# A graph network with routed experts and two attention layers on one core: output bias in bf16 parts, attention rows from two banks, one square root, and each strong result added ahead of the next group sum

## What is computed

```python
h = x @ W_in + b_in                                   # 6250 x 256
for l in range(3):
    agg = segment_sum(h[src], dst) / deg
    logits = concatenate([h, agg]) @ router_W[l] + router_b[l]
    gates = softmax of the two largest of 8 logits, 0 elsewhere
    weak = relu(agg @ weak_W[l] + weak_b[l])          # 4 experts, 256 -> 256
    sh = relu(agg @ strong_W1[l] + strong_b1[l])      # 4 experts, 256 -> 512
    strong = sh @ strong_W2[l] + strong_b2[l]         # 512 -> 256
    moe = sum over the 8 experts of gate * result
    h = h + sigmoid(h @ conf_W[l] + conf_b[l]) * moe
x1 = layernorm(x + h @ W_out + b_out)                 # 6250 x 128
y = gat(elu(gat(x1, 4 heads of 32)), 1 head of 128)   # attention over the edges
return layernorm(x1 + y)
```

## Time and profile before

| | us |
|---|---|
| median of 3 runs | 8288.14 |
| lowest, highest | 8262.08, 8299.24 |
| the profiled execution | 8303.62 |
| its span in the trace | 8302.0 |
| busy in the span: POOL, PE, DVE, ACT | 4148.2, 3593.2, 3261.6, 1275.6 |
| mean granted PE clock | 0.681 |

### The profile page before, as it was taken

How to read it: one execution, slowest core, us unless ns; L and a number is a source line. 1 busy time by engine, 2 the same in 40 slices (tenths; PEclk the granted TensorE clock), 3 DMA queues, 4 the chain that set the end, 5 groups by cost and what they waited for, 6 DMA issues and landing times.

```text
span 8302.0 us, 58045 instructions
## 1 busy us (share of the span) xinstructions
PE 3593.2 (43%) x11996; PEld 2114.2 (25%) x11996; DVE 3261.6 (39%) x6283; ACT 1275.6 (15%) x2738; POOL 4148.2 (50%) x4324
## 2 busy tenths in 40 slices
PE   3127777676567666665666666662000000000000
PEld 2124333344433333334433333331000000000000
DVE  2224444343333333333333333324444444454553
ACT  1002222222122222221222222221000000000000
POOL 5654445454544344445344444334655565666555
PEclk6558888788677877776778787876555555555555
DMA  2332222222322222223121212112212121211111
GB/s 66 88 107 65 72 64 76 72 74 64 94 63 63 58 68 62 68 63 96 54 62 56 61 55 62 55 33 48 50 45 47 47 48 39 46 46 45 45 43 42
DMA packets 259368, 500.84 MB, mean 60 GB/s; under 512 B 104427, under 2 KB 146340, under 8 KB 258874
## 3 DMA queue, kind: packets, MB, share of 16 engines
q0 software_dynamic: 176592, 446.04, 20.5%
q1 hardware_dynamic: 56234, 33.56, 1.5%
q10 hardware_dynamic: 26432, 20.02, 0.7%
HBM read 464.44 MB, written 34.88 MB: 60 GB/s over the span
## 4 chain that ended last, share of the span: by engine, by line
PE 33%; issue 24%; another core or an unknown queue 18%; DVEq 10%; DVE 6%; ACT 3%; POOL 1%; ACTq 1%; DMA 0%; SPq 0%; POOLq 0%
PE ps_w1a L1942 7%; PE ps_w1b L1942 6%; PE ps_gate L1967 5%; PE ps_wide L1967 4%; PE ps_weak_a L1954 3%; PE ps_weak_b L1954 3%; DVE ps_wide L1382 2%; DVEq L1414 2%; PE ps_weak_a L1926 1%; DVEq L1427 1%; DVEq L1354 1%; DVEq L1424 1%; ACT weak L1611 1%; DVEq L363 1%
## 5 line engine op out<-in xcount | busy, mean ns | idle before, releaser
L655 POOL DMA_INDIRECT ring<-hidden_tab,stage x2400 | 2316.0, 965 | 2792.0 <-DVE ps_wide L967 1779.5
L655 POOL DMA_INDIRECT ring<-gat_tab,stage x1600 | 1530.4, 956 | 1143.7 <-issue 651.0
L973 DVE TENSOR_TENSOR ps_wide<-ps_wide,ring 128x1024 f32<-128x1024 f32 x418 | 516.2, 1235 | 544.3 <-issue 537.1
L1942 PE MATMUL ps_w1a<-agg_team_t,wbuf 128*128 128x512 f32 (+1 forms) x1248 | 632.5, 625 | 201.1 <-ACT strong L1590 108.6
L1942 PE MATMUL ps_w1b<-agg_team_t,wbuf 128*128 128x512 f32 (+1 forms) x1248 | 591.8, 595 | 51.5 <-issue 46.9
L1967 PE MATMUL ps_gate<-wbuf,strong 128*128 128x256 f32 x2400 | 578.3, 387 | 14.4 <-issue 14.2
L1967 PE MATMUL ps_wide<-wbuf,strong 128*128 128x256 f32 x2304 | 555.8, 384 | 62.7 <-issue 62.2
L2078 PE MATMUL ps_w1a<-ident,agg_team_t 128*128 128x128 f32 x28 | 7.8, 434 | 1242.9 <-DVE agg_team_t L1460 666.8
L1967 PEld LDWEIGHTS ps_gate<-wbuf,strong 128*128 128x128 f32 x2400 | 443.2, 195 | 131.8 <-issue 65.8
L1967 PEld LDWEIGHTS ps_wide<-wbuf,strong 128*128 128x128 f32 x2304 | 419.8, 192 | 143.7 <-issue 66.2
L977 DVE SCALAR_TENSOR_TENSOR ps_wide<-ring,before_cut,ps_wide 128x256 f32<-128x256 f32 x556 | 243.5, 485 | 478.4 <-issue 462.1
(11 more groups left out here) (409 smaller groups left out, 4659.7 us busy)
## 6 DMA issues: line engine op xcount, KB each, us to landing
ring<-hidden_tab,stage POOLq DMA_INDIRECT x2400
ring<-gat_tab,stage POOLq DMA_INDIRECT x1600
hidden_tab<-h_res ACTq DMA_DIRECT2D x24, 512.0 KB, 3.0
hidden_tab<-h_res SPq DMA_DIRECT2D x12, 512.0 KB
wbuf<-in_L_gnn_strong_W SPq DMA_DIRECT2D x6, 1024.0 KB
wbuf<-in_L_gnn_strong_W SPq DMA_DIRECT2D x12, 512.0 KB
gat_tab<-h_res ACTq DMA_DIRECT2D x19, 272.0 KB
wbuf<-in_L_gnn_weak_W SPq DMA_DIRECT2D x6, 512.0 KB
```

What stands on the lines that cost most here:

```text
L655: return pool.indirect_dma_start(out=ring[:, b, 0:width], out_offset=None, in_=table, in_offset=bass.IndirectOffsetOnAxis(ap=stage[:, half ...
L973: nc.vector.tensor_tensor(wide_s, wide_s, rows(u), ALU.add).then_inc(ring_free, 1)
L1942: last = mm(ps_w1[c % 2][:, 0:size * P], w1_w[:, k, s, c * P:(c + 1) * P], agg_team_t[:, k, 0:size * P], start=k == 0, stop=k == 1)
```

## The change

Four things, in five engines' programs:

1. **Output bias.** `b_out` is no longer multiplied in fp32 by a row of ones. It is loaded on three partitions (`bias_out`), split by `bias_parts` into three bf16 rows of a 128 x 128 tile `out_parts` that is otherwise 0, and each group's projection starts with one bf16 product of ones with it.
2. **Attention rows.** The eight score columns are a product of their own into a second bank, so the features of four groups fill one bank. ACT copies a batch in three activations and drains once. The stores are issued by SP in its pass for the first attention layer, each after `row_done`.
3. **One square root.** ACT computes Sqrt instead of Ln and Exp, after the last team's state copies instead of before them, and DVE takes the reciprocal.
4. **Order on DVE.** In every team step of all three expert layers `add_strong(s - 1)` and a drain stand ahead of `gather_next(s)`. In the last-but-one and last steps (few or no next groups) the same lines run with little or nothing to sum.

```diff
@@ parameters, SP
-        ones_row = sb("ones_row", [1, P])
-        b_out_r = sb("b_out_r", [1, IN])
+        out_parts = sb("out_parts", [P, IN], BF16)
+        bias_out = agg_flat[:, P:P + IN]
-        PAR_DMAS = 4 + 5 + 4 * LAYERS + 2 * (2 + 2 * HEADS)
+        PAR_DMAS = 3 + 8 + 4 * LAYERS + 2 * (2 + 2 * HEADS)
-            par(b_out_r[:], b_out.rearrange("(a n) -> a n", a=1))
             for row in PART_ROWS:
                 par(bias_in[row:row + 1, :], b_in.rearrange("(a n) -> a n", a=1))
+                par(bias_out[row:row + 1, :], b_out.rearrange("(a n) -> a n", a=1))
@@ SP, pass r of the places
+                if r == LAYERS:
+                    for b in range(BATCHES):
+                        n = min(BATCH, GROUPS - b * BATCH)
+                        sp.wait_ge(row_done, b * BATCH + n)
+                        sp.dma_start(rows_of_team(gat_tab[0], b, n), gat_rows[:, b * BATCH:b * BATCH + n, :]).then_inc(table_done, 16)
@@ POOL
+            nc.gpsimd.memset(out_parts[:], 0.0)
-            nc.gpsimd.memset(ones_row[:], 1.0)
@@ DVE
             dve.drain().then_inc(s_parts, 1)
+            bias_parts(bias_out, out_parts)
+            dve.drain().then_inc(s_out_parts, 1)
...
                     for s in range(1, NS):
-                        at = gather_next(s, at)
                         between()
                         add_strong(r, q, s - 1, size)
+                        dve.drain()
+                        at = gather_next(s, at)
                         between()
...
+            def rstds(count, first, last):
+                dve.wait_ge(std_ready, count)
+                nc.vector.reciprocal(ln_r[:, 2, first:last], ln_r[:, 1, first:last])
+                dve.drain()
+            rstds(1, 0, EARLY)
             normalize(0)
...
-            dve.wait_ge(rstd_ready, 2)
+            rstds(2, EARLY, GROUPS)
             normalize(TEAMS - 1)
@@ ACT
-            def all_rstd(count, first, last):
+            def all_std(count, first, last):
                 act.wait_ge(var_ready, count)
-                nc.scalar.activation(ln_r[:, 1, first:last], ln_r[:, 0, first:last], ACT.Ln)
-                act.drain()
-                nc.scalar.activation(ln_r[:, 2, first:last], ln_r[:, 1, first:last], ACT.Exp, scale=-0.5).then_inc(rstd_ready, 1)
+                nc.scalar.activation(ln_r[:, 1, first:last], ln_r[:, 0, first:last], ACT.Sqrt).then_inc(std_ready, 1)
...
+                made, scores = (ps_w1, ps_weak)[b % 2]
+                act.wait_ge(row_ready, b * BATCH + n)
...
+                act.drain().then_inc(row_done, n)
-            all_rstd(1, 0, EARLY)
             take_state(LAYERS - 1, TEAMS, 1)
             take_state_t(TEAMS, 1)
+            all_std(1, 0, EARLY)
             take_z(TEAMS, 1)
@@ PE
-                    mm(o, ones_row[:], b_out_r[:], start=True, stop=False)
+                    mm(o, ones_b[:], out_parts[:], start=True, stop=False)
...
-                    mm(o, h_team_t[:, b % 2, j * P:(j + 1) * P], gat_w[0][:], start=True, stop=True).then_inc(row_ready, 1)
+                    mm(made[:, j * P:(j + 1) * P], h_team_t[:, b % 2, j * P:(j + 1) * P], gat_w[0][:, 0:P], start=True, stop=True)
+                    mm(scores[:, j * 2 * HEADS:(j + 1) * 2 * HEADS], h_team_t[:, b % 2, j * P:(j + 1) * P], gat_w[0][:, P:P + 2 * HEADS],
+                       start=True, stop=True).then_inc(row_ready, 1)
```

More of the change, by code:

```diff
@@ L346, in gnn_kernel @@
         weak_ready, weak_copied, weak_added, h_done = sem("weak_ready"), sem("weak_copied"), sem("weak_added"), sem("h_done")
[L347 to L349 removed]
+        s_parts, s_strong_parts, s_out_parts = sem("s_parts"), sem("s_strong_parts"), sem("s_out_parts")
+        hout_ready, houtT_ready, houtT_copied, b_out_ready, z_ready, var_ready, std_ready, rstd_ready = (sem(n) for n in (
+            "hout_ready", "houtT_ready", "houtT_copied", "b_out_ready", "z_ready", "var_ready", "std_ready", "rstd_ready"))
         x1_ready, x1T_ready, x1T_copied, row_ready, row_done = (sem(n) for n in (
@@ L1717, in batch_rows @@
             def batch_rows(b):
-                for half in range(2):
-                    g = b * BATCH + 2 * half
-                    n = min(2, GROUPS - g)
-                    if n > 0:
-                        act.wait_ge(row_ready, g + n)
-                        made = (ps_w1, ps_weak)[b % 2][half][:, 0:n * (P + 2 * HEADS)].rearrange("p (j n) -> p j n", n=P + 2 * HEADS)
-                        nc.scalar.activation(gat_rows[:, g:g + n, 0:HEADS * HC].rearrange("p j (h c) -> p j h c", c=HC)[:, :, :, 0:HID],
-                                             made[:, :, 0:P].rearrange("p j (h c) -> p j h c", c=HID), ACT.Copy)
-                        nc.scalar.activation(gat_rows[:, g:g + n, GW - HEADS:GW], made[:, :, P:P + HEADS], ACT.Copy)
-                        nc.scalar.activation(ad[0][:, g:g + n, :], made[:, :, P + HEADS:P + 2 * HEADS], ACT.Copy)
-                        act.drain().then_inc(row_done, n)
-                act.wait_ge(row_done, min((b + 1) * BATCH, GROUPS))
-                those = slice(b * BATCH, min((b + 1) * BATCH, GROUPS))
-                act.dma_start(rows_of_team(gat_tab[0], b, those.stop - those.start), gat_rows[:, those, :]).then_inc(table_done, 16)
-            all_rstd(1, 0, EARLY)
+                n = min(BATCH, GROUPS - b * BATCH)
+                those = slice(b * BATCH, b * BATCH + n)
+                made, scores = (ps_w1, ps_weak)[b % 2]
+                scores = scores[:, 0:n * 2 * HEADS].rearrange("p (j n) -> p j n", n=2 * HEADS)
+                act.wait_ge(row_ready, b * BATCH + n)
+                nc.scalar.activation(gat_rows[:, those, 0:HEADS * HC].rearrange("p j (h c) -> p j h c", c=HC)[:, :, :, 0:HID],
+                                     made[:, 0:n * P].rearrange("p (j h c) -> p j h c", h=HEADS, c=HID), ACT.Copy)
+                nc.scalar.activation(gat_rows[:, those, GW - HEADS:GW], scores[:, :, 0:HEADS], ACT.Copy)
+                nc.scalar.activation(ad[0][:, those, :], scores[:, :, HEADS:2 * HEADS], ACT.Copy)
+                act.drain().then_inc(row_done, n)
             take_state(LAYERS - 1, TEAMS, 1)
             take_state_t(TEAMS, 1)
+            all_std(1, 0, EARLY)
             take_z(TEAMS, 1)
```

12 lines of the change are left out of this document (4 added, 8 removed).

## The result

The changed kernel takes 8143.8 us (median of 4 runs, 8140.2 to 8153.0) against 8278.8 before on the same chips (4 runs, 8262.1 to 8299.2): a ratio of 0.984, 95% interval 0.981 to 0.986. That is 135 us less. The forecast was 8135 us within 7930 to 8340. The profiled execution took 8152.95 us.

The account below looks back on a forecast made before the run. No engine bounds the whole; long gather runs on POOL slow issue and signals. Terms -110 (order, layers 1 and 2), -33 (layer 0), -7 (bias), 0 (rows), -5 (square root) sum to -155 us from 8288.1: 8133, say 8135, range 7930 to 8340.

Parts of the forecast that it names:

- What bounds: Expert layer steps: no engine bounds as a whole; signals and issue are slow during long runs of gathers on POOL.
- The order on DVE: Team steps: adding before summing breaks the first gather run; 5 us a step gained in layers 1 and 2, 110 us.
- Layer 0: First expert layer: many steps already have short runs, so 3 us for 11 steps, 33 us gained.
- the bound of 17.7 us: Most a step could win, from two layer 0 steps of 114.3 and 132.0 us with first runs of 24 and 36.
- The add ahead: DVE's add and drain before each of three sums: 1 to 4.5 us a step lost if the run isn't broken.
- Output bias: Layer 2 projection: one bf16 product saves PE 0.3 us in each of 49 groups; half counted, 7 us gained.
- Rows of the attention table: Table stage: ACT's saving against PE's extra records, taken as 0, bounds -7 to +5 us.
- One square root: Table stage on ACT: fewer table loads than with Ln and Exp, -5 us, bounds 0 to -7.
- Rival 1: Team steps: signals still pass 15 us into the run, which isn't broken; slower, near 8360 us; chance 0.16.
- Rival 2: Expert layers: run broken, but the gain is given back at the step's end before the router; 8276 us; chance 0.14.
- Rival 3: Team steps: short runs end before slowing anything; 33 steps gain 12 to 17 us, 7720 to 7890 us; chance 0.08.
- the ranking distance: Layer 2 sign of being right: rankings lie 130 to 137 us apart instead of 142.

Follow-up runs that it names:

- before_pause4: The kernel before, DVE untouched, with POOL waiting after every four gathers in the expert layers until they have landed: 7561.9 us, 0.911.
- bias_only: The kernel before with the bf16 output bias alone: 8335.8 us, 1.005.
- order_only: The kernel before with only the new DVE order, each strong result added ahead of the next group sum: 8150.8 us, 0.983.
- sqrt_only: The kernel before with only the single Sqrt on ACT and the reciprocal on DVE: 8182.7 us, 0.998.
- wait_s2: The kernel before with one added DVE wait, for the second strong result ahead of the sum of group 2, adds unmoved: 7852.4 us, 0.946.
- pause8_all: The kernel before with a POOL pause at every eighth gather, also at the ring turn's start and in the attention layers: 6987.0 us, 0.853.
- s2_only: The kernel before with the new DVE order for s = 2 alone, the old for the others: 7918.0 us, 0.956.
- no_order: The changed kernel with the old DVE order, so output bias, attention rows and square root alone: 8352.2 us, 1.008.

## Why the prediction was right, and where it was off

*What bounds.* Right. The slow issue during long runs of gathers was the thing to look at, and `before_pause4` bears it out with DVE untouched.

*The order on DVE.* Predicted 5 us a step in layers 1 and 2, 110 us; measured 171 (99.3 and 72.1), 7.8 a step. The working named the run of 16 to 20 gathers (20), the add near 4838, 48 us after the ranking (51.7), the sum of group 2 done 11 us sooner (9.0, by its last instruction against the ranking), and the fourth run of gathers, which didn't come: the sums of groups 3 and 0 share a third run of 28. In the step shown group 0's sum starts 8.8 us sooner, is slowed by that run and ends only 1.5 us sooner. But I gave back 3 us a step to a last run that would meet the next router, and it doesn't reach it: from the end of that sum to the ranking it is 11.1 us instead of 14.7. This step gained 5.1 us, others more; layer 1 kept 8 us a step.

*Layer 0.* I took 33 us; it was 6. My comparison of two steps there was misread, and with it the bound of 17.7 us. An earlier step, 739.0 to 854.5, takes 115.6 us although its first run is one of 32:

```profile
758.50:800.50 42.00, 31.25 (x32) 0.77 0.39 105
```

What goes with the length of these steps is what follows the first run: 16 and 8 gathers apart in the short ones of 115.6 and 115.8 us, 20 at once in that of 132.0. The new order took this break away in some steps (115.8 became 118.5, 114.3 became 123.9) while it shortened the long ones (126.3 to 114.2, 132.0 to 119.4): one effect against the other.

*The add ahead.* The working carries it as 1 to 2 us for s = 1 and 3 us for s = 2 (add at 4838, sum from 4841), and as 1 to 4.5 us a step where the run isn't broken. It is 2.13 each, three in a step, 6.4. It took 249 of the 384 us that the waits alone give. So the net gain came out near the forecast with both of its sides larger than I took them.

*Output bias.* Predicted -7. With the old order it isn't seen: layer 2 of `bias_only` is 1610.1 us against 1609.6. With the new one the changed kernel's layer 2 is 17 us below that of `order_only`, about the 15 us of PE time that I had worked out, but from one execution of each, on different chips. The cost of 57 us in layer 0 was in no term; its bound of +4 came from reading each instruction's own place, and what failed is the step "One more memset on POOL for one removed: nothing" and its like, that a shift without a cost has no effect.

*Rows of the attention table.* The step that failed: "ACT's cycle of about 2.2 us a batch shrinks by 0.6 or so and PE's grows to about the same 2.2". PE's went from 2.20 to 4.16 from one batch to the next, as ACT's copies of the features show, each of which waits for PE:

```profile
5465.20 0.60 ACT L1735 ACTIVATE h_res<-ps_w1a 128x512 f32<-128x512 f32 x1 [2.56 <-PE ps_w1b L2073]
...
5469.36 0.60 ACT L1735 ACTIVATE h_res<-ps_weak_a 128x512 f32<-128x512 f32 x1 [2.56 <-PE ps_weak_b L2073]
```

I had added records at the full clock; the stage ran at half of it. With `sqrt_only` as the form without it, the part costs 22 us, 17 over the bound of +5.

*One square root.* Predicted -5, measured -7 in its stage. The load for the next Exp, which the Trainium skill asks for (page "ScalarE: Activation LUTs", section "Table sets: the hidden batching unit"), came 28 times, not once, and cost nothing that the times show.

*Rivals.* Rival 1, signals still passing 15 us into the run, didn't happen: the first half of the result reached ACT at 4814.40, behind the run's end. Rival 2, all given back at the end of the step, is excluded by layer 1. Rival 3, all of 17.7 us a step, needed what the change doesn't do, but its size was there to be had: `wait_s2` gains 16.5 us a step in layer 1 and 15.4 in layer 2, and `pause8_all`, with 1172.2 us for the 12 steps of layer 2, is 27 us a step below `sqrt_only` on the same chips.

*The attention layers.* +25 us in the profiled executions was in no term. Over the thirteen kernels profiled with the same attention code, the stretch from the first attention gather to the end lay between 2621 us (`s2_only`) and 2664 (`no_order`), with and without the table loads, 2628 in the kernel before and 2643 in `order_only`. So I don't put it down to any part; what moves it stays open.

*The sum.* That 8143.8 lies so near 8135 is in part luck. Layers gained 177 us where my terms for order and bias had 150; what follows them lost 40 where I had -5; the start gave 11 that no term had. Inside the layers 61 us too little in layers 1 and 2 stood against 27 too much in layer 0. Of the signs that I named, those of the layers came, the ranking distance at its edge (137.0); the table stage, which was to be 5 us shorter, is 15 longer.

## What to carry to other kernels

When several engines show idle time put down to "issue" or "remote" in the same stretch, look for what they share before pricing any of their instructions: here it was the length of an unbroken run of gathers, or how densely gathers lie, and a deliberate pause of 2.6 us in every eight gathers was worth 15%. When a reordering gains, ask whether the order or the wait that it brings does the work, and try the wait alone; here it was worth about three times the order. A product split for the sake of a bank costs records of its own (one of 8 columns took as long as 0.29 us from its start to the next), and they are priced at the clock at which the stage then runs, not by their columns.

## What the runs showed of the hardware that I hadn't expected

- Issue on PE and DVE and the signals to ACT slow down together once POOL has gathered without a pause for some 15 us (in the kernel before from 4809.7 to 4825), and recover about 3 us after the last gather (4857.1, and PE's and ACT's issue at 4860). A single gap of 2.88 us in a run brought DVE's fast issue back but not the signals to ACT. With regular pauses of 2.60 us after four gathers ACT's largest "remote" waits are gone in most of layer 2; after eight, in `pause8_all`, 49.3 and 39.3 us are left of them, none over 7.7. All this though the mean rate of gathers is higher (65 from 4023 to 4123 in `pause8_all` against 64 in 142 us before).
- PE's clock stayed at 0.50 for 33 us in which its records fill all of the time, in a stage of alternating 128- and 8-column products with a weight load each, and was 1.00 in the same stage with 136-column products and less busy time.
- A change that touches no instruction of a step can move it by 12 us, when the step's length hangs on which wait happens to fall into a run.
